# Negated maxima, ranks from one difference, shorter roots, one distance table, and a new order on every engine

## The reference

```
# block 0, attention: 16 heads of 8, a distance bias per head
slopes = 2.0 ** (8.0 * arange(0, -H, -1) / H)
scores = q @ k.T / sqrt(Hd) - slopes[:, None, None] * abs(pos[None, :] - pos[:, None])
x = norm(x + softmax(scores) @ v @ W_out.T + b_out)
# block 0, experts: 8 and a shared one; weights are the top 2 of a softmax over 8 gate logits
x = norm(x + sum_e combine[:, e] * ((silu(x @ w1[e] + b1[e]) * (x @ w3[e] + b3[e])) @ w2[e] + b2[e]) + shared)
# block 1, attention over 16 shifts: score = q[n] . k[n - shift] + pos_bias, softmax, sum of v[n - shift], gated
x = norm(x + gathered * sigmoid(x @ w_gate + b_gate) @ w_out + b_out)
# block 1, experts: softmax over the top 2 gate logits of 8
x = norm(x + sum_e w_full[:, e] * (x @ expert_w[e].T))
# norm(x) = (x - mean) / sqrt(var + 1e-5)
```

## Time and profile before

| what | us |
|---|---|
| median of 3 runs | 1725.61 (1722.67 to 1727.79) |
| profiled execution | 1721.39 |
| its span | 1719.6 |
| PE, DVE, ACT, POOL busy | 1465.4, 1297.0, 913.0, 882.3 |
| C1.prod on POOL, line 1068 | 349.1 |
| A1.max on DVE, line 993 | 338.5 |
| exponentials of A2 on ACT, line 701 | 277.0 |
| M.neg on DVE, line 1036 | 32.5 |

### The profile page before, as it was taken

How to read it: one execution, slowest core, us unless ns; L and a number is a source line. 1 busy time by engine, 2 the same in 40 slices (tenths; PEclk the granted TensorE clock), 3 DMA queues, 4 the chain that set the end, 5 groups by cost and what they waited for, 6 DMA issues and landing times.

```text
span 1719.6 us, 36166 instructions
## 1 busy us (share of the span) xinstructions
PE 1465.4 (85%) x12928; PEld 1134.0 (66%) x12928; DVE 1297.0 (75%) x3466; ACT 913.0 (53%) x1868; POOL 882.3 (51%) x772
## 2 busy tenths in 40 slices
...
GB/s 120 98 93 95 113 131 126 152 144 131 138 132 134 128 115 138 152 148 128 139 136 132 126 114 139 152 130 146 124 147 125 119 126 145 148 87 108 83 111 31
DMA packets 88983, 214.26 MB, mean 125 GB/s; under 512 B 10499, under 2 KB 67075, under 8 KB 67459
## 3 DMA queue, kind: packets, MB, share of 16 engines
...
## 4 chain that ended last, share of the span: by engine, by line
PE 39%; DVE 24%; issue 18%; POOL 11%; ACT 3%; DMA 3%; SPq 1%; DVEq 0%; POOLq 0%; ACTq 0%
POOL wb L1059 8%; PE b L508 7%; PE bPV L529 6%; DVE mx L993 5%; PE bS L546 4%; PE b L567 4%; PE bTU L558 4%; PE bTU L559 3%; POOL prod L1068 2%; DVE wb L962 2%; DVE wb L911 2%; PE bS L549 2%; DVE mneg L1036 2%; DVE gat L975 1%; DVE wb L969 1%
## 5 line engine op out<-in xcount | busy, mean ns | idle before, releaser
L1059 POOL TENSOR_TENSOR wb<-wb 128x1024 f32<-128x1024 f32 x64 | 150.6, 2354 | 498.0 <-DVE wb L911 498.0
L993 DVE TENSOR_REDUCE mx<-bS 128x2 f32<-128x512 f32 x512 | 338.5, 683 | 57.2 <-PE bS L549 55.7
L1068 POOL TENSOR_TENSOR prod<-kC,qC 128x512 f32<-128x512 f32 x256 | 349.1, 1399 | 37.2 <-ACT kC L670 37.2
L701 ACT ACTIVATE P<-bTU 128x512 f32<-128x512 f32 x512 | 277.0, 607 | 106.0 <-PE bTU L481 79.1
L1093 POOL TENSOR_TENSOR h<-ub,gBcb 128x256 f32<-128x256 f32 x256 | 184.0, 730 | 188.1 <-DVE ub L1006 153.5
L546 PE MATMUL bS<-stack 96*128 96x256 bf16 x1024 | 217.8, 280 | 35.3 <-DVE mx L993 14.8
L478 PE MATMUL bTU<-stack 97*128 97x256 bf16 x1024 | 227.3, 275 | 5.5 <-ACT P L701 2.5
L481 PE MATMUL bTU<-dist,identh 128*128 128x128 f16 x1024 | 206.5, 220 | 0.0
L558 PE MATMUL bTU<-x1T,w 128*128 128x256 f32 x576 | 184.1, 402 | 24.6 <-DVE h L1006 24.6
L549 PE MATMUL bS<-dist,identh 128*128 128x128 f16 x1024 | 197.1, 223 | 0.0
L710 ACT ACTIVATE sil<-bTU,b 128x256 f32<-128x256 f32 x288 | 130.1, 475 | 104.6 <-PE bTU L559 56.4
...
## 6 DMA issues: line engine op xcount, KB each, us to landing
...
stack<-d_parts SPq DMA_DIRECT2D x192, 192.0 KB
...
```

Source lines behind the costliest of these rows:

```text
L701: act_f(P[k % 8][:].rearrange("p a b -> p (a b)"), bTU[turn_bank("ST", k)][:], ACT.Exp).then_inc(actA2.done("exp", k), 1)
L993: v.tensor_reduce(mx[:, :, k], bS[k % 2][:].rearrange("p (a b) -> p a b", a=TT), op=ALU.max, axis=AX.X).then_inc(dveA1.done("max", k), 1)
L1059: tt_(pv[:, 8 * n:8 * n + 4, :], pv[:, 8 * n:8 * n + 4, :], pv[:, 8 * n + 4:8 * n + 8, :], ALU.add).then_inc(poolC2.done("add", n), 1)
L1068: tt_(prod[:, 2 * p:2 * p + 2, :], shifted(kC, p), qC[:].unsqueeze(1).to_broadcast([128, 2, T]), ALU.mult).then_inc(poolC1.done("prod", p), 1)
```

## The change

Five things. A1.max writes the negated maximum as bf16 itself, and M.neg and its buffer go. G.rank takes the differences of all pairs once and compares them with a table (`least`: 0, or the negated smallest normal number for an earlier index), in place of two comparisons, a product and an addition. The inverse root has another first guess, one Newton step with other constants and one step of higher order, seven instructions instead of nine. The scores are computed divided by the head's slope: q is scaled by a column `qs0` that holds it, the exponential multiplies by the slope again, and one table of whole numbers, exact in f16, serves all heads; the low half and its product go. And every engine's list in `ORDER` is new.

```diff
-        A1.qk A1.v B2.z D2.y.0 A2.ST.0 D2.y.1 A2.ST.1 A2.ST.2 A2.ST.3 A2.ST.4 A2.ST.5 A2.ST.6 A2.PV.0 A2.ST.7
+        A1.qk B2.z A1.v D2.y.0 D2.y.1 A2.ST.0 A2.ST.1 A2.ST.2 A2.ST.3 A2.ST.4 A2.ST.5 A2.ST.6 A2.ST.7 A2.PV.0 B.xT
...
-        dist = sb("dist", [128, H, 2, 128], H16)
+        dist = sb("dist", [128, 128], H16)
...
-                            last_part = h % 2 == 0
-                            i = mm(o[:, c], identh[:], dist[:, h, 0, :], start=False, stop=last_part)
-                            if not last_part:
-                                i = mm(o[:, c], identh[:], dist[:, h, 1, :], start=False, stop=True)
+                            i = mm(o[:, c], identh[:], dist[:], start=False, stop=True)
...
-                              scale=q_scale).then_inc(actA1.done("q"), 1)
+                              scale=qs0[:, 0:1]).then_inc(actA1.done("q"), 1)
...
-                        act_f(P[k % 8][:].rearrange("p a b -> p (a b)"), bTU[turn_bank("ST", k)][:], ACT.Exp).then_inc(actA2.done("exp", k), 1)
+                        act_f(P[k % 8][:].rearrange("p a b -> p (a b)"), bTU[turn_bank("ST", k)][:], ACT.Exp,
+                              scale=SLOPES[head(k)]).then_inc(actA2.done("exp", k), 1)
...
+                if 2 in parts:
+                    dve.wait_ge(dveN.sem, dveN.count(e, "nt", 2))
+                    v.tensor_tensor(ns, nr, nr, ALU.mult).then_inc(dveN.done("nt", 3), 1)
+                    dve.wait_ge(dveN.sem, dveN.count(e, "nt", 3))
+                    v.tensor_tensor(ns, ns, nv, ALU.mult).then_inc(dveN.done("nt", 4), 1)
+                    dve.wait_ge(dveN.sem, dveN.count(e, "nt", 4))
+                    v.scalar_tensor_tensor(ns, ns, -ROOT_C, ns, ALU.add, ALU.mult).then_inc(dveN.done("nt", 5), 1)
+                    dve.wait_ge(dveN.sem, dveN.count(e, "nt", 5))
+                    v.scalar_tensor_tensor(nr, ns, ROOT_D, nr, ALU.add, ALU.mult).then_inc(dveN.done("nt", 6), 1)
...
-                v.tensor_tensor(o[0], lj, li, ALU.is_gt).then_inc(dveG.done("gt"), 1)
+                v.tensor_tensor(o[1], lj, li, ALU.subtract).then_inc(dveG.done("dif"), 1)
...
-                v.tensor_tensor(o[1], lj, li, ALU.is_equal).then_inc(dveG.done("eq"), 1)
-                dve.wait_ge(dveG.sem, dveG.count(e, "eq"))
-                v.tensor_tensor(geq[:, m], geq[:, m], tri[:].unsqueeze(1).to_broadcast([128, n, TT * E * E]),
-                                ALU.mult).then_inc(dveG.done("eqt"), 1)
-                dve.wait_ge(dveG.sem, dveG.count(e, "eqt"))
-                v.tensor_tensor(ggt[:, m], ggt[:, m], geq[:, m], ALU.add).then_inc(dveG.done("add"), 1)
-                dve.wait_ge(dveG.sem, dveG.count(e, "add"))
+                dve.wait_ge(dveG.sem, dveG.count(e, "dif"))
+                v.tensor_tensor(ggt[:, m], gdf[:, m], least[:].unsqueeze(1).to_broadcast([128, n, TT * E * E]),
+                                ALU.is_gt).then_inc(dveG.done("gt"), 1)
+                dve.wait_ge(dveG.sem, dveG.count(e, "gt"))
...
-                            dve.wait_ge(dveM.sem, dveM.count(e - 1, "neg"))
-                        v.tensor_reduce(mx[:, :, k], bS[k % 2][:].rearrange("p (a b) -> p a b", a=TT), op=ALU.max,
-                                        axis=AX.X).then_inc(dveA1.done("max", k), 1)
+                            dve.wait_ge(peM.sem, peM.count(e - 1, "mT"))
+                        v.tensor_reduce(mneg[:, :, k], bS[k % 2][:].rearrange("p (a b) -> p a b", a=TT), op=ALU.max,
+                                        axis=AX.X, negate=True).then_inc(dveA1.done("max", k), 1)
...
-                    if what == "M.neg" and (e := r["M"]) is not None:
-                        dve.wait_ge(dveA1.sem, dveA1.count(e, "max", 15))
-                        dve.wait_ge(peM.sem, peM.count(e - 1, "mT"))
-                        v.tensor_scalar(mneg[:], mx[:], -1.0, None, ALU.mult).then_inc(dveM.done("neg"), 1)
```

More of the change, by code:

```diff
@@ L27 @@
 ROW_M = 96
+SLOPES = [2.0 ** (-8.0 * h / H) for h in range(H)]
 LAG = {"X": -1, "A1": 0, "M": 0, "A2": 1, "A3": 1, "A3n": 2, "B": 2, "B2": 3, "C1": 3, "C2": 4, "C2n": 5,
@@ L50 @@
+        A2.ST.8 C1.xT D.xT A2.ST.9 A2.ST.10 B.lg D.lg A2.ST.11 A2.PV.1 C1.qk A2.ST.12 A2.ST.13 A2.ST.14 A2.PV.2
+        A2.ST.15 B.cT B.ab.0 A1.S.0 A1.S.1 A2.PV.3 A1.S.2 A1.S.3 B.ab.1 A1.S.4 C1.vg A1.S.5 B.ab.2 A3.pT A1.S.6
+        A1.S.7 D.cT B.ab.3 C2.out A1.S.8 A1.S.9 B.ab.4 A1.S.10 C1.sc A1.S.11 B.ab.5 C1.scT B.ab.6 A1.S.12 A1.S.13
+        B.ab.7 A3.aT B.z A1.S.14 C1.wT A1.S.15 A3.out B.ab.8 M.mT""",
     "act": """
-        A1.qk A2.exp.0 A2.exp.1 A2.exp.2 A2.exp.3 A2.exp.4 A2.exp.5 A2.exp.6 A3n.nm A2.exp.7 C2n.nm B.xT B2.nm D.xT
@@ L55 @@
     "dve": """
-        A1.rest A1.v A1.mid A1.lo B2.res D2.res N.root.0 N.root.1 N.root.2 N.root.3 C2.pv.0 C2.pv.1 C2.pv.2 C2.pv.3
-        G.rank C2.pv.4 G.weigh C2.pv.5 C2.pv.6 C2.pv.7 C2.add.0 A1.max.0 A1.max.1 C2.add.1 A1.max.2 C2.add.2 A3.rec
-        B.wu.0 C2.gt A1.max.3 B.wu.1 A1.max.4 A3.num A1.max.5 A1.max.6 B.wu.2 A1.max.7 A1.max.8 C2.res A1.max.9
-        B.wu.3 A1.max.10 B.wu.4 A1.max.11 A1.max.12 C1.mx B.wu.5 B.wu.6 A1.max.13 A1.max.14 C1.sum B.wu.7 A1.max.15
-        M.neg A3.res B.wu.8""",
+        A1.rest A1.v A1.mid B2.res A1.lo D2.res N.root.0 N.root.1 N.root.2 C2.pv.0 N.root.3 C2.pv.1 C2.pv.2 C2.pv.3
@@ L61 @@
+        C2.pv.4 C2.pv.5 C2.pv.6 G.rank C2.pv.7 G.weigh C2.add.0 A1.max.0 A1.max.1 C2.add.1 A1.max.2 A1.max.3
+        C2.add.2 A1.max.4 B.wu.0 C2.gt A1.max.5 A1.max.6 A1.max.7 B.wu.1 A1.max.8 B.wu.2 C2.res A1.max.9 B.wu.3
+        B.wu.4 A3.rec A1.max.10 A1.max.11 A3.num C1.mx B.wu.5 B.wu.6 A1.max.12 A1.max.13 C1.sum B.wu.7 A1.max.14
+        A1.max.15 A3.res B.wu.8""",
     "pool": """
         C2.add.0 C2.add.1 C1.prod.0 C1.prod.1 C1.prod.2 C1.prod.3 C1.prod.4 C1.prod.5 C1.prod.6 C1.prod.7 B.h.1
-        B.h.2 B.h.3 A3.xbo B.h.4 D.xs.0 B.h.5 B.h.6 D.xs.1 B.h.7 D.xs.2 B.h.8 C2.xb D.xs.3""",
+        B.h.2 B.h.3 C2.xb B.h.4 A3.xbo B.h.5 D.xs.0 D.xs.1 B.h.6 B.h.7 D.xs.2 B.h.8 D.xs.3""",
@@ L64 @@
     "sp": """
-        A1.part.0 A1.part.1 A1.part.2 C2.wb A1.rows.0 A1.rows.1 A1.rows.2 B.cT B.cb X.xT D.cT A3.x D.cb C1.dw M.m
-        C1.wb D2.out""",
+        C2.wb A1.part.0 A1.part.1 A1.part.2 A1.rows.0 A1.rows.1 A1.rows.2 B.cT A3.x B.cb X.xT D.cT D.cb D2.out C1.dw
+        M.m C1.wb""",
 }
@@ L205, in network @@
         LN = "res bn*2 ag*2"
-        GATE = "cp gmx gt sub eq eqt add rank sel sum rec c"
+        GATE = "cp gmx dif sub gt rank sel sum rec c"
         peA1 = steps("peA1", "qk v S*16")
@@ L225, in network @@
         dveA1 = steps("dveA1", "rest v mid lo max*16")
-        dveM = steps("dveM", "neg")
         dveA3 = steps("dveA3", "rec num*2 " + LN)
```

92 lines of the change are left out of this document (40 added, 52 removed).

## The result

The changed kernel is 0.8% slower: 1737.42 us in the median of ten executions (1731.92 to 1759.69), against 1724.52 of the kernel before on the same chip (1721.50 to 1727.79). The ratio is 1.0078, with a 95% interval of 1.0052 to 1.0105; it is taken without the longest execution of the ten, which counts as a slow one. The forecast was 1665 with a range of 1635 to 1702. The profiled execution took 1736.13 us, its span 1734.1.

A forecast was written before the change was run, and what follows sets the result against it. Bound by a front chain over four engines and a nearly gapless DVE back; 1.8 us a pass over 28 passes (50), plus 3 and 6, less 0.5 at the start, is 59 off 1725.6: 1665, range 1635 to 1702.

The forecast's parts named there:

- the order of the front: Front of a pass: PE waits 1.7 us at B.xT and 0.8 at ST.8; first maximum at 24.0, gain 1.1.
- the back of the pass: From the first maximum on: the same DVE work as before, with 0.5 us of idle time where PE is late.
- Sizing the stretch at 0.5: C2.pv.4 to pv.6 on DVE, stretched beside POOL's first addition, cost 0.5 us more, so C2.add.0 ends at 23.4.
- the negated maxima: End of a pass: M.neg goes, a gain of 0.8 us a pass (bounds 0.4 and 1.2).
- roots and ranks: DVE steps: two root steps fewer save 0.4 us, a comparison and an addition fewer in the ranks save 0.9.
- rival D: A1.S.0 waits for stack because C2.wb delays d_parts: 2.0 us a pass slower, 1773; chance 0.07.
- the table's 0.9 of TensorE: Whole-number table: 16 f16 products a pass go at 0.06 us each, 0.9 us of PE a pass.
- the check from PE's side: PE's busy 44.5 us a pass, less 0.9, plus 3.3 of front waits, is 46.9: a gain of 1.6.
- A: Rival: the back frees up too, DVE alone setting the pass; 2.8 us a pass gained, 1639; chance 0.12.
- B: Rival: late norms and C2.pv.0 waiting for wb eat most gain; 0.6 to 0.9 a pass, 1700 to 1690; chance 0.16.
- C: Rival: no difference, waits only change places and PE's 0.9 is lost to late exps; 1720 to 1731; chance 0.05.
- the signs of being wrong: A1.S.0 waits for stack, C2.pv.0 waits for wb, passes under 46 us, or A1.max waits for PE over 1 us a pass.

The follow-up runs named there:

- e3_fill: Changed kernel with four unread TensorE products more a pass, three ahead of the wait at B.xT and one ahead of ST.8; 1694.22 us, ratio 0.981.
- e2_order_only: Kernel before the change with the new lists of all engines, its instructions kept, M.neg ahead of A3.res; 1798.04 us, ratio 1.042.
- e1_old_order: Changed kernel with the old order lists of all engines, M.neg left out; 1658.65 us, ratio 0.961 to the kernel before.
- e10_pv_behind_rank: Changed kernel with C2.pv.4 to pv.6 put back behind the ranks on VectorE; 1796.43 us, ratio 1.042 to the kernel before.
- e11_table_only: Kernel before the change with the one whole-number distance table alone, low halves gone; 1726.46 us, ratio 1.0014.
- e7_swap_norms: Changed instructions in the old order, with norm C2n ahead of A2.exp.7 and A3n behind it on ScalarE; 1699.55 us, ratio 0.985.

## Why the prediction was wrong

The sum said 1662.4 for the profiled execution, which took 1736.1: 73.7 us more. By the starts of the passes:

| stretch | forecast | measured | off |
|---|---|---|---|
| passes 7 to 30, clock | nothing | 1177.1 - 24 x 47.37 | 40 |
| passes 7 to 30, at full clock | 24 x 46.7 | 24 x 47.37 | 16 |
| start of pass 7, against 301.4 before | -8 | +6.2 | 14 |
| pass 31 and the last six, 254.2 before | -8 | -4.8 | 3 |

**The step that failed** is in the order of the front: "PE waits some 1.7 and 0.8 us there, where it waited 0.57, and one long wait is moved, not removed". The place and, within 0.3, the size of both waits were right, and they were counted at their own length only. The sum was made at the clock of 1.00 of the earlier trace rows, and no rival had it fall. Filling the waits took 43 us off without any other step changed (`e3_fill`), so that the 40 us are shown to be the clock. `e2_order_only` has the falls without the other edits. This step alone turns the sign: with the waits filled the kernel is at 1690 to 1694, faster than before and inside the range.

**The second step** is "the back of the pass is the same DVE work, with 0.5 of idle time where PE is late". The back grew by 1.16, from longer instructions beside POOL (0.70 and 0.49, less 0.5 elsewhere) and 0.44 more of waits for scores. It is the new order that does this. In `e1_old_order`, with the same instructions, VectorE's first and last maximum of the pass from 341.43 on are:

```profile
365.48 1.29 DVE L1000 TENSOR_REDUCE mneg<-bS 128x2 bf16<-128x512 f32 x2
...
386.46 0.70 DVE L1000 TENSOR_REDUCE mneg<-bS 128x2 bf16<-128x512 f32 x1
```

The first is at 24.05 and the back takes 20.98, as it did before the change. So of the 1.42 that the front gained, 1.13 came with the instructions and 0.29 with the order, and the order lost 1.17 in the back.

C2.add.0 was stretched too, 2.19 for 1.23: POOL's C1.prod starts at once behind its addition (329.12, ahead of C2.add.0 at 329.20), since C1.qk is earlier on TensorE; before, it started 0.59 after the addition, waiting for ScalarE's copy, and C2.add.0 was in first. The forecast counted pv.4 to pv.6 beside POOL's first addition (the six of L918 took 6.07 together), and forgot that the same holds for every later instruction of this kind. G.weigh's last one (L879), on 32 elements, took 1.92 beside the second addition, where it took 0.19. So nothing is left of the 1.5 us of idle time that was forecast ahead of C2.add.0. That POOL is beside them is read from the timelines; that it is the cause is shown for the products L918 alone, where the longest goes from 2862 to 694 ns in `e10_pv_behind_rank`.

By the Trainium skill, "SBUF — State Buffer", section "Who interferes with whom", a VectorE instruction with two SBUF inputs and a POOL instruction that reads SBUF exclude each other. The trace agrees: the products of L918 take 677 ns at their shortest and 2862 at their longest, which is the length of POOL's addition (2.35) and some. The reductions from PSUM (L1000) never took over 702 ns, as the section says of them. Sizing the stretch at 0.5 for three products left the total at the front right (max.0 at 24.0 forecast, 23.76 measured), because it lay in idle time.

**Right**: the negated maxima (0.8 forecast, 1.0 alone, 0.93 at the pass's end), `n_b` at 10.95 (10.93), B.xT at 12.75, ST.8 at 14.0 (13.9), S.0 at 23.6 (23.2), roots and ranks at 1.3 (1.25, by difference only), and stack's rows in time (rival D needed an end at 25.4; the waits are 0.7 us in all). **Wrong in size and in worth**: the table's 0.9 of TensorE, used in the check from PE's side, was 0.5 of busy time in `e11_table_only` and nothing of the pass. The 3.3 of front waits in that check stand in no row; TensorE's waits in the pass of 47.4 are 3.9. **The first passes**: 14 us. In pass 0 the first A1.S waits 14.12, where it waited 12.42. Pass 1 waits 5.03 for stack instead of 3.62, and passes 4 and 5, with clocks of 0.50 for 7 and 10 us, take 47.49 and 49.03 instead of 46.64 and 46.29; the forecast had gains there.

**The rivals.** A (the back frees up) is opposite to what came. B gave 1690 to 1700, which is where the kernel stands with its clock repaired, but by another mechanism: the front gained more than forecast, and the back lost. Its wait for `wb` is there too (17.9 us in 21 places of the stretch 300 to 1400), but at C2.pv.4, the first of the second half, and not at C2.pv.0, so that `n_b` isn't late. C and D fail on the passes of 47.4. Of the signs of being wrong one came true: A1.max waits for PE for 53 us in the stretch, over 2 a pass, though only 0.88 in the pass of 47.4. The slower outcome, given 0.07, came by a way that wasn't in the list.

Open: why 1.44 and 0.75 bring the clock down in twelve passes in groups (9 to 12, 16 to 19, 27 to 30) and not in the others, which have the same waits; and why a single 1.64 (`e7_swap_norms`) does so once. VectorE's wait for `wb`, which differs from pass to pass, doesn't tell them apart: it is 1.61 in pass 26, which keeps its clock, and 0.45 in pass 16, which doesn't. The 0.9 between the full-clock passes of the two orders lies in the back; how the 0.8 of it that isn't POOL's list divides among the other lists no run shows.
